# Local attention's key product a tile sooner and ahead of the values, query and key weights loaded apart, and the memory layer's beginning and end in another order

## The reference, cut to what matters

```python
qkv = x @ Wqkv                      # x: tokens x 128, q, k, v: 1024 each
q = l2norm(q) * qs                  # norm over the 64 of a head
k = l2norm(k) * ksc
q = q * cos * scale + rotate_half(q) * sin * scale
k = k * cos / scale + rotate_half(k) * sin / scale
out = local_attention(q, k, v)      # softmax over 64 keys
x = x + out @ Wo
x = x + ffn_layer(x)                # layer norm, gated gelu
```

```python
k, v, q = (causal_dwconv(hidden @ W.T, w, b) for each of k, v, q)
alpha, eta, theta = means of sigmoid / sigmoid / softplus of hidden @ W.T
for chunks of 64 tokens:            # 32 rounds, one behind the other
    gradients of the memory's loss, clipped by norm; state and weights scanned; retrieval
out = retrieved @ Wo.T
out = out * rsqrt(mean(out * out) + 1e-6) * norm_g
return out * (hidden @ gW.T + gb)
```

## Time and profile before

| | us |
|---|---|
| runs of the kernel | 4520.35, 4527.34, 4534.48 (median 4527.34) |
| profiled execution, its own time | 4526.65 |
| profiled execution, span | 4524.6 |
| TensorE busy | 3985.9 (88%) |
| VectorE busy | 3143.6 (69%) |
| ScalarE busy | 2543.4 (56%) |
| GpSimd busy | 1193.2 (26%) |

### The profile page before, as it was taken

How to read it: one execution, slowest core, us unless ns; L and a number is a source line. 1 busy time by engine, 2 the same in 40 slices (tenths; PEclk the granted TensorE clock), 3 DMA queues, 4 the chain that set the end, 5 groups by cost and what they waited for, 6 DMA issues and landing times.

```text
span 4524.6 us, 114197 instructions
## 1 busy us (share of the span) xinstructions
PE 3985.9 (88%) x46878; PEld 2213.8 (49%) x46974; DVE 3143.6 (69%) x5193; ACT 2543.4 (56%) x3754; POOL 1193.2 (26%) x1015
## 2 busy tenths in 40 slices
PE   3689999989999999767688999999997599999997
PEld 1255555555555555535454555555553233333333
DVE  7688888888888888565514666666664676767772
ACT  4357666666666666552224555555553266666674
POOL 0266656656566656300000000000000011111110
PEclk6899999999999999865578999999998699999998
DMA  0122223222232222101000000000001200000000
GB/s 18 59 67 78 68 65 81 72 70 72 63 82 69 72 73 65 46 14 24 16 9 16 4 4 4 4 3 2 4 1 53 71 19 19 19 19 19 18 1 15
DMA packets 85358, 166.79 MB, mean 37 GB/s; under 512 B 23336, under 2 KB 37336, under 8 KB 83568
## 3 DMA queue, kind: packets, MB, share of 16 engines
q1 hardware_dynamic: 84816, 159.13, 13.5%
HBM read 40.60 MB, written 8.52 MB: 11 GB/s over the span
## 4 chain that ended last, share of the span: by engine, by line
PE 48%; issue 19%; POOL 14%; DVE 12%; ACT 5%; DMA 1%; SPq 1%; POOLq 0%; DVEq 0%; ACTq 0%
POOL arena L977 7%; POOL arena L981 6%; PE banks L1276 6%; PE banks L2209 5%; PE banks L1259 4%; PE banks L1247 4%; ACT arena L2347 2%; PE banks L520 2%; PE banks L2183 2%; PE banks L2167 2%; PE banks L1295 1%; DVE arena L853 1%; DVE arena L1429 1%; PE banks L2190 1%; PE banks L2187 1%
## 5 line engine op out<-in xcount | busy, mean ns | idle before, releaser
L2421 DVE TENSOR_REDUCE arena<-banks 128x2 f32<-128x1024 f32 x512 | 614.2, 1223 | 277.7 <-PE banks L2174 141.0
L2347 ACT ACTIVATE arena<-banks 128x1024 f32<-128x1024 f32 x512 | 522.6, 1025 | 281.5 <-PE banks L2190 147.2
L977 POOL TENSOR_TENSOR arena<-arena 128x512 f32<-128x512 f32 x384 | 424.2, 1126 | 643.6 <-DVE arena L862 636.1
L981 POOL TENSOR_TENSOR arena<-arena 128x1024 f32<-128x1024 f32 x192 | 533.2, 2777 | 15.1
L1429 DVE CUSTOM_DVE_ANT_0 arena<-arena,banks 128x512 f32<-128x512 f32 (+3 forms) x640 | 361.8, 603 | 234.3 <-issue 233.0
L1372 ACT ACTIVATE arena<-banks 128x512 f32<-128x512 f32 (+3 forms) x320 | 170.1, 532 | 409.5 <-PE banks L1259 408.8
L520 PE MATMUL banks<-arena 128*128 128x512 f32 x768 | 367.3, 622 | 37.4 <-ACT arena L701 16.5
L2209 PE MATMUL banks<-arena 128*32 128x256 f32 x4096 | 335.7, 394 | 13.2 <-issue 7.8
L1364 ACT ACTIVATE arena<-arena 128x128 f32<-128x128 f32 (+15 forms) x256 | 328.5, 1285 | 11.5 <-DVE arena L1441 6.5
L2522 POOL MEMSET arena<- 128x8 f32 x1 | 0.1, 105 | 1252.1 <-DVE xn L180 1252.1
L1247 PE MATMUL banks<-arena 64*128 64x512 f32 (+3 forms) x1280 | 322.8, 582 | 4.7 <-issue 3.7
(11 more groups left out here) (432 smaller groups left out, 7499.9 us busy)
## 6 DMA issues: line engine op xcount, KB each, us to landing
arena<-arena SPq DMA_DIRECT2D x768, 64.0 KB
arena<-arena SPq DMA_DIRECT2D x96, 384.0 KB, 3.6
arena<-arena SPq DMA_DIRECT2D x96, 128.0 KB, 3.4
arena<-in_lf_wqkv SPq DMA_DIRECT2D x6, 1024.0 KB, 5.7
arena<-features_k SPq DMA_DIRECT2D x32, 128.0 KB
arena<-arena SPq DMA_DIRECT2D x8, 512.0 KB
arena<-features_q SPq DMA_DIRECT2D x16, 216.0 KB
arena<-in_lf_wqkv SPq DMA_DIRECT2D x6, 512.0 KB, 3.9
```

The source lines that it names most:

```text
L977: nc.gpsimd.tensor_tensor(r[:, :, e * H2:(e + 1) * H2], q[:, j, :, (1 - e) * H2:(2 - e) * H2], s[:, j, 1, e * H2:(e + 1) * H2].unsqueeze(1 ...
L981: nc.gpsimd.tensor_tensor(a, a, lf_rb, ALU.add).then_inc(S("lf_rot" + x), 1)
L2347: nc.scalar.activation(bi_PT[n % 4], PS[:, 2 * bi_slot("S", n):2 * bi_slot("S", n) + 2].rearrange("p a b -> p (a b)"), ACT.Exp).then_inc(S ...
L2421: nc.vector.tensor_reduce(bi_max[j % 2][:, t, :, c], PS[:, 2 * slot:2 * slot + 2], AX.X, ALU.max).then_inc(S("bi_mx"), 1)
```

## The change

In local attention `qk` becomes `k` and `q`. The k of tile s+1 is issued in step s, behind the feed-forward piece and the wait for `scale(s)`, ahead of the first half of the values; only k of tile 0 stands in its own step. The q of tile s opens step s. The squares of k of tile s+1 come in step s on ScalarE, between the feed-forward piece and `keep_o`; their sums on VectorE close step s. `up`'s second product (or `mean`) moves ahead of the wait for `scale`. The weights of q, k and v come as three inputs, and q's and k's are loaded by two transfers with a semaphore each. In the memory layer the copies of k, v, q move ahead of the sigmoids, two large memsets and a small one go from VectorE to GpSimd, and at the end Sqrt with VectorE's reciprocal becomes Ln and Exp on ScalarE.

```diff
+            def k(n, l):
+                if n % NB == 0:
+                    pe.wait_ge(S("lf_wk_in"), (l + n // NB) * 16 + 16)
                 pe.wait_ge(S("lf_xb"), l * 2 * NB + (2 * n + 2))
                 if n >= 1:
                     pe.wait_ge(S("lf_qn"), l * NB + n)
-                for j in (2, 3, 0, 1):
-                    if j == 0:
-                        if n >= 4:
-                            pe.wait_ge(S("lf_ot"), l * NB + (n - 3))
+                for j in (2, 3):
                     m = nc.tensor.matmul(PS[:, j], lf_xb[:, n % 4], ck(lf_wqk, j), start=True, stop=True)
+                m.then_inc(S("lf_k"), 1)
+            def q(n, l):
+                if n % NB == 0:
+                    pe.wait_ge(S("lf_wq_in"), (l + n // NB) * 16 + 16)
+                if n >= 4:
+                    pe.wait_ge(S("lf_ot"), l * NB + (n - 3))
+                for j in range(2):
+                    m = nc.tensor.matmul(PS[:, j], lf_xb[:, n % 4], ck(lf_wqk, j), start=True, stop=True)
+                m.then_inc(S("lf_q"), 1)
...
                 if more and s == NB - 1:
+                    sp.wait_ge(S("lf_k"), l * NB + NB)
+                    lf_load_k(sp, following)
                     sp.wait_ge(S("lf_q"), l * NB + NB)
-                    lf_load_qk(sp, following)
+                    lf_load_q(sp, following)
...
                 elif ffn:
                     gate(c, j - 1, l)
+                if lf_live(s + 1, end):
+                    squares(s + 1, l, 1)
                 if lf_live(s - 3, end):
                     keep_o(s - 3, l)
...
                 if lf_live(s - 4, end):
                     add(s - 4, l)
+                if lf_live(s + 1, end):
+                    sums(s + 1, l, 1)
...
-                nc.scalar.activation(ck(tt_ors, c), PS[:, c], ACT.Sqrt, bias=tt_eps[:, 0:1]).then_inc(S("tt_ostd"), 1)
+                nc.scalar.activation(ck(tt_ors, c), PS[:, c], ACT.Ln, bias=tt_eps[:, 0:1]).then_inc(S("tt_oln"), 1)
+                act.wait_ge(S("tt_oln"), c + 1)
+                nc.scalar.activation(ck(tt_ors, c), ck(tt_ors, c), ACT.Exp, scale=-0.5).then_inc(S("tt_ostd"), 1)
...
+            nc.gpsimd.memset(tt_gp[0:64], 0.0).then_inc(S("tt_zero"), 1)
             pool.wait_ge(S("tt_zero"), 1)
+            nc.gpsimd.memset(tt_rp[32:64], 0.0).then_inc(S("tt_zero"), 1)
```

More of the change, by code:

```diff
@@ L445, in lf_sp @@
             first = bass.ds(0, 1)
-            lf_load_qk(sp, first)
+            lf_load_k(sp, first)
+            lf_load_q(sp, first)
             lf_load_scales(sp, first)
@@ L651, in step @@
                 b, ending = lf_chunk_before(s, end)
+                if s == 0:
+                    k(0, l)
                 if lf_live(s, end):
-                    qk(s, l)
+                    q(s, l)
                 if lf_live(s - 2, end):
@@ L678, in step @@
                     mean(c, l)
+                if lf_live(s - 3, end):
+                    values_ready(s - 3, l, end)
+                if lf_live(s + 1, end):
+                    k(s + 1, l)
                 if lf_live(s - 3, end):
@@ L701, in block_in, with squares @@
                 nc.scalar.activation(lf_xb[DH:P, n % 4], lf_y[DH:P, t * P:(t + 1) * P], ACT.Copy).then_inc(S("lf_xb"), 1)
[L703 to L708, removed]
+            def squares(n, l, j):
+                x = "qk"[j]
+                act.wait_ge(S("lf_" + x), l * NB + (n + 1))
+                if n >= 1:
+                    act.wait_ge(S("lf_red" + x), l * NB + n)
+                nc.scalar.activation(ck(lf_sqb, j, INNER), PS[:, 2 * j:2 * j + 2].rearrange("p a b -> p (a b)"), ACT.Square).then_inc(S("lf_sq" + x), 1)
             def norms(n, l):
@@ L791, in step @@
                     shifted(c, l)
+                if s == 0:
+                    squares(0, l, 1)
                 if lf_live(s, end):
-                    squares(s, l)
+                    squares(s, l, 0)
                 if s > 8 and lf_chunk(s - 1, end)[2] and j != 1:
@@ L836, in lf_dve, with sums @@
             dve.wait_ge(S("lf_zeroed"), 1)
+            def sums(n, l, j):
+                x = "qk"[j]
+                dve.wait_ge(S("lf_sq" + x), l * NB + (n + 1))
+                nc.vector.tensor_reduce(lf_n2[:, j * HEADS:(j + 1) * HEADS, 0], ck(lf_sqb, j, INNER).rearrange("p (a b) -> p a b", b=DH), AX.X, ALU.add).then_inc(S("lf_red" + x), 1)
             def norm(n, l):
-                for j, x in ((1, "k"), (0, "q")):
-                    dve.wait_ge(S("lf_sq" + x), l * NB + (n + 1))
-                    nc.vector.tensor_reduce(lf_n2[:, j * HEADS:(j + 1) * HEADS, 0], ck(lf_sqb, j, INNER).rearrange("p (a b) -> p a b", b=DH), AX.X, ALU.add).then_inc(S("lf_red" + x), 1)
+                sums(n, l, 0)
                 dve.wait_ge(S("lf_redq"), l * NB + (n + 1))
@@ L927, in step @@
                     product(c, j - 2, l)
+                if s == 0:
+                    sums(0, l, 1)
                 if lf_live(s, end):
@@ L1768, in tt_act @@
             for c in range(NCH):
+                act.wait_ge(S("tt_kvq"), c + 1)
+                nc.scalar.activation(ck(tt_xp[:, 3:T + 3], c)[0:96], PS[0:96, c], ACT.Copy).then_inc(S("tt_xp"), 1)
+            for c in range(NCH):
                 act.wait_ge(S("tt_gates"), c + 1)
@@ L1884, in tt_dve @@
             nc.vector.memset(tt_n, 0.0).then_inc(S("tt_scan"), 1)
+            dve.wait_ge(S("tt_zero"), 2)
             dve.wait_ge(S("tt_nth"), 1)
@@ L2610, in layout @@
     D, H, DH, W = 6, 16, 64, 32
-    o["lf_wqkv"] = f["L0_ffn_Wqkv"]
+    o["lf_wq"], o["lf_wk"], o["lf_wv"] = (f["L0_ffn_Wqkv"][:, :, n * H * DH:(n + 1) * H * DH] for n in range(3))
     o["lf_wo"] = f["L0_ffn_Wo"].reshape(D, 8, P, P).transpose(0, 2, 1, 3)
```

29 lines of the change are left out of this document (11 added, 18 removed).

## The result

The changed kernel takes 4620.35 us (4 runs, 4617.61 to 4622.52), the kernel before 4530.91 on the same chip (4 runs, 4520.35 to 4535.26): ratio 1.0204, 95% interval 1.0191 to 1.0217. It is slower by 89.4 us, where +117.3 had been forecast. The sign and the mechanism are as forecast; of the sizes several are off, and some of them cancel.

A forecast was written before the change was run, and what follows sets the result against it. TensorE was taken as the bound, its in-order list and waits lengthening local attention one for one. Terms: 125.6 - 2.1 - 6.2 = +117.3 us on 4526.65, giving 4644 us; range 4572 to 4690.

The forecast's parts named there:

- q behind the values: Local attention: q waits for `keep_o` to empty its banks, no longer covered by k's products; +1.32 us in 92 steps.
- More after j = 0: Step after j = 0: k's squares stand ahead of `keep_o` on ScalarE; +1.3 us more, q at 2.62 instead of 1.32.
- The second `up`: Feed-forward part of local attention: its wait for `scale` goes, 3 x 0.29 = 0.87 us saved per group.
- These three cancel in a group: Four-step group of local attention: gains 6.58 us, loses 0.87, +5.71; over 22 groups +125.6.
- Tiles 4 to 7 and the loop's branches: Tiles 4 to 7 save no `scale` wait, +5.3; at four branches TensorE is already late, so no stall, -5.3.
- The stage's end: End of local attention: no term of its own; 22 groups of tiles 8 onward and tiles 4 to 7 were counted.
- Weights: Last step of a layer: k's weights may load late; taken as 0, with +19.5 us over five layers as the end.
- Memory's beginning and end: Memory layer: earlier copies of k, v, q, -2.1 us; Ln and Exp in place of roots and reciprocals, -6.2 us.
- The clock's share at the beginning: Memory's 16 TensorE products: a higher clock after shorter idle time could save up to 7 us; none taken.
- VectorE as the bound: Local attention: VectorE's list ends 0.5 us after the scores in 88 steps, +44 us, 4688 us; chance 0.10.
- The stall taken out of `turn_k`'s wait: Local attention: late q shortens `turn_k`'s 62.4 us of waits instead of adding to them; 4582 us, chance 0.08.
- Faster by k's early place: VectorE carries the period, moving k's sums frees `scale`, q's stall lies in idle time; 4500 us, chance 0.06.

The follow-up runs named there:

- Exchanging two calls: Changed kernel, but on ScalarE the squares of the next k stand behind `keep_o` instead of ahead of it: 4576.11 us, ratio 1.0116 against the kernel before.
- with `project` last: Changed kernel, but `project` stands behind the values, directly ahead of q, and k's squares behind `keep_o`: 4468.54 us, ratio 0.9862 against the kernel before.

## Why the prediction was right, and where its sizes were off

- **q behind the values.** Forecast 1.32 us a step, measured 1.22 (2.29 - 1.07): `keep_o` ends at 835.22 and q starts at 835.27, so handing back took 0.05 us and not 0.14. The mechanism is shown from three sides: covered by `project` the wait goes (121.2 us to 1.2), lengthened by 1.07 us it lengthens the step by all of that, and VectorE's maximum still waits for the scores meanwhile.
- **More after j = 0.** Forecast 2.62, measured 2.28, for the reason given (the squares ahead of `keep_o`). What the forecast missed was TensorE's clock: most products behind these waits of 2.2 us ran at the lower level, which adds about 1 us (TensorE's busy time in these steps rose from 18.20 to 19.28 us). The steps grew by 3.32 us. Exchanging two calls gave 44 us back.
- **The second `up`.** Forecast -0.29 a step from the wait's rows. The steps grew by 0.75, not by 1.22, so some 0.47 went, and the experiment on its own gave 0.52. The term was sized by the idle time in brackets; from start to start it is larger. Tested alone it was 1.1 us a group, near the forecast's 0.87, because the steps after j = 0 gave 0.44 back.
- **These three cancel in a group**: 3 x 0.75 + 3.32 = +5.57, forecast +5.71. The group came out right for reasons that partly were not.
- **Tiles 4 to 7 and the loop's branches.** Forecast +5.3 and -5.3, measured +8.0 (with the first steps and the last) and -4.5.
- **The stage's end.** Forecast at nothing, measured -10.5. This is the step that failed by most: the 22 groups were counted and the emptying of the pipeline was not. There the second `up` had stood behind the copies of the windows (the wait of 4.03 us on DMA above, and one of 4.41 behind it), and it now runs in that time. The experiment that only moved three quarters of this product shows -6.9 in the same stretch. The other 3.6 are not tested apart; part of them is clock, as values, `project` and values behind the first of these waits took 7.4 us before (1883.82 to 1891.20) and take 4.2 now (1998.75 to 2002.92).
- **Weights.** Taken as 0, measured 0.9 us in all. The prediction called v's 512 KB half the size of this load; k's own is 512 KB as well, and lands after 4.3 us on the median.
- **Memory's beginning and end.** Forecast -2.1 and -6.2, measured -3.9 and -6.1. The clock's share at the beginning had been bounded by -7 and taken as 0; it is -1.5, and the copies gave 2.4. One of the eight traces with this edit does not have the 1.5.
- **The rest.** Forecast at nothing; the layers behind memory took 5.8 us less in this profile, within the scatter of the ten traces.

Span by span: +106.6 (forecast +125.6) - 9.7 (memory, with its rounds; forecast -8.3) - 5.8 = +91.1, and the spans differ by 4615.7 - 4524.6 = 91.1. Most of what the forecast was too high by is the stage's end; the nearness of the group's sum is luck in part.

Of the rivals, VectorE as the bound did not come here, as its maximum waits for the scores 63 times between 600 and 1800 us, and 42 times before; whether it comes once the stall is gone is open. The stall taken out of `turn_k`'s wait is refuted: 0.69 us each before, 0.76 after. Faster by k's early place is refuted for this order. With `keep_o` covered the same edits give 0.9862, -59.0 us, but of these the moved `up` alone gives some 28.7 and the memory layer's edits 13.8. How the other 16.5 are shared by k's place, `project`'s and the steps at the loop's branch, no run separates.

## What to carry to other kernels

Before an instruction is moved ahead, ask what it was covering where it stood: k's 1.85 us hid a 1.04 us copy and its hand-over, and any other 2 us of TensorE's own work (`project`) hid it as well. Weigh a wait from the start of one instruction to the start of the next, not by the idle time alone, look where the waits come back when one is removed, and count the lead and the emptying of a pipeline besides its steady groups. On an in-order engine, work that is ready and in nobody's way still must not stand ahead of the one copy that another engine waits for.

## What the runs showed of the hardware that was not expected

- TensorE's granted clock fell behind most single waits of 2.21 to 2.33 us in a stretch that was otherwise nearly full: q's products took 3.01 to 3.02 us on the mean there (71 of 88 over 2.3 us), and 1.98 to 2.00 behind waits of 1.16 to 1.31 us (1 of 154). Doubling a 1.04 us copy cost 195.5 / 92 = 2.1 us per tile. With 92 waits of 2.2 us or more the mean clock of local attention was 0.92 instead of 0.98.
- Waits of 0.29 us on the mean in the middle of a row of TensorE's products cost 0.52 us an ordinary step from start to start; one of 0.35 cost 0.60.
- A table load costs ScalarE its 1.28 us and 0.03 more from one activation's end to the next one's start (1.31), also with eight loads at the memory layer's end; the seven that were taken out gave only 6.8 us, as VectorE's work had lain beside them.
- Idle time of TensorE that no semaphore explains moved with the order of the instructions: 14.8 us at q in four steps of the changed kernel; with `project` last 7.8 there, and 12.9 inside the values, five of them at the same record in each pass.
- GpSimd's memsets took 5.40 us (64x6368) and 10.33 us (32x12288), 0.85 and 0.84 ns an element, beside other work.
